# Sending the shift rows of the attention's query stacks from SBUF to SBUF on ScalarE's queue

## The chip, the cores and the metric

One core of a Trainium2 chip runs the whole kernel. The metric is the device time of one execution in microseconds (us); the time before is the median of three runs.

## The reference

The kernel computes a small image tower: a Haar tokenizer, attention with a layer norm, a mixture of eight experts (two per token), a cosine attention block with its feed-forward part, and a second mixture of experts. The change touches only the attention of the first layer, 16 images of 256 tokens with 256 features, 16 heads of 16:

```python
Q, K, V = (proj(Wq, bq), proj(Wk, bk), proj(Wv, bv))
scale = 1.0 / jnp.sqrt(jnp.float32(hd))
scores = jnp.einsum('bhqd,bhkd->bhqk', Q, K) * scale
attn = jax.nn.softmax(scores, axis=-1)
out = jnp.einsum('bhqk,bhkd->bhqd', attn, V)
out = out.transpose(0, 2, 1, 3).reshape(B, S, D)
return out @ Wo.T + bo
```

Its result is added to the input, normed, and routed: logits, the two best experts, a softmax over the two, and each token's rank within its expert.

## The kernel before

The function `attention` runs one image per turn, as a software pipeline of some five turns; all five engines go through the same table `STEPS`, and each takes the steps that it has a function for, in that order. A step's letter gives the image: `n2` is the image of this turn (its load and transpose), `f` the one before (projections), `n` two back (first score pass), `t` three back (second pass, probabilities, values), `p` four back (output projection, norm, routing) and `o` five back (ranks and rows to the experts). So consecutive steps of one engine belong to different images.

The heads are worked in pairs: 8 pairs an image, each with two heads g on partitions 64g and up. q and k are split into a high part and a rest in `parts`; SP writes these to DRAM (`split`, steps qw and kw, L537) and reads them back, stacked three times 16 rows per head, into `qs` and `ks` (`stack`, steps stq and stk, L548): twelve transfers of 128 KB an image, all on SP's queue, the semaphore `stack_in` at the end.

p1_j (L672, TensorE) makes the scores of pair j with 48 rows, queries on the partitions, and VectorE takes their row maximum (L863). After four pairs, step shift_0 or shift_1 (L871, L873, VectorE) makes the negated maxima and their rounding rest. These are to stand in rows 48 and 49 of each query stack, so that the second pass with 50 rows subtracts them. The way there, before: step sw_half transposes them on TensorE into bank[0] (L680), ScalarE copies the 16 x 256 result to `shiftT` (L805), SP writes that to DRAM (`shift_store`, L554) and, in step sr_half, reads it into the stacks (`shift_rows`, L560, two transfers of 8 KB). sw_0 and sr_0 stand late in the turn of p1; sw_1 and sr_1 stand in the next turn.

p2_j (L693, TensorE) makes the scores again, keys on the partitions; p2_0 and p2_4 wait for `shift_in` of their half, and each p2 waits for `prob_ok` of the one before, as the two score banks are one buffer. ScalarE exponentiates (L811). av_k (L705) multiplies with the values; ScalarE copies the result (heads, L818). Routing (step route) is a chain of small VectorE instructions with ScalarE's exponential L834 in it; the ranks follow in step rk (L757 to L761, TensorE, bank[0]). The projections q and k are L650 (q in bank[1], k in bank[0]), with ScalarE's L789 (parts_q, parts_k) behind. Each user of a bank waits for the reader of the use before it (`claim`, `hold`), so who shares bank[0] (rk, sw, k, ot_0) also sets who waits.

Of the kernel before, what the change touches and what calls it, by code (L numbers as in the profile page):

```python
# [6 lines left out]
F32 = mybir.dt.float32  # L7
# [5 lines left out]
ACT = mybir.ActivationFunctionType  # L13
# [3 lines left out]
IMAGES, SEQ, D = 16, 256, 256  # L17
# [15 lines left out]
STACK = 3 * HD  # L33
# [370 lines left out]
def attention(nc, a, s, h0_d, h1_d, rows0_d, ident, before, ones, iota8, cnt, gates0, expert0, rank0, minus_half):  # L404
# [5 lines left out]
    def sb(name, shape, dt=F32):  # L410
        return ctx.enter_context(nc.sbuf_tensor(name, shape, dt))
# [3 lines left out]
    PAIRS = HEADS // 2  # L415
    KROWS = STACK + 2
    RING = 3
# [2 lines left out]
    h0_v = h0_d.rearrange("(i t p) d -> i p t d", t=TPI, p=P)  # L420
    h1_v = h1_d.rearrange("(i t p) d -> i p t d", t=TPI, p=P)
    split_d = [[nc.dram_tensor(f"split_d{u}{n}", (2, 2 * P, SEQ), F32, kind="Internal").ap() for n in "qk"] for u in range(2)]
    shift_d = [nc.dram_tensor(f"shift_d{half}", (2, 2, PAIRS // 2 * SEQ), F32, kind="Internal").ap() for half in range(2)]

    with ctx:
        raw = sb("raw", [P, 4, 2, D])
# [14 lines left out]
        vx = [sb(f"vx{u}", [P, TPI, HEADS, 32]) for u in range(RING)]  # L441
        top = sb("top_a", [P, PAIRS, 2, TPI])
        shift = sb("shift", [P, 2, TPI, 2, 2, PAIRS // 2], F32R)
        shiftT = sb("shiftT", [2 * PAIRS, SEQ])
        prob = sb("prob", [P, 4, 2, TPI, SEQ])
        heads4 = [sb(f"heads4_{u}", [P, SEQ]) for u in range(2)]
        rden = sb("rden", [P, 16])
# [14 lines left out]
        rk = sb("rk", [P, TPI, E])  # L462
# [6 lines left out]
        av_bank = ctx.enter_context(nc.psum_tensor("av_bank", [P, 512], F32))  # L469

        names = ("w_in w_ps w_ok b_in ks_ok bv_ok bo_ps bo_ok filled xt_ps xT_ok q_ps k_ps v_ps qh_ok kh_ok q_ok k_ok v_ok q_out k_out "
                 "s1_ok s1_used shift_ok sT_ps sT_ok sT_out s2_ok prob_ok quad_ok ot_ok on_ps att_ok aT_ps aT_ok o_ps res_ok xb_ok var_ok "
                 "rstd_ok h1_ok hT_ps hT_ok lg_ps lg_ok away_ok ex_ok pick_ok rk_ps rk_ok row_ok").split()
        q = {n: sem("a_" + n) for n in names}
        x_in, h1_out, shift_in = (sem.pair("a_" + n) for n in ("x_in", "h1_out", "shift_in"))
# [3 lines left out]
        def head(k, j):  # L479
            return 8 * (j // 2) + 2 * k + j % 2  # L480

        STEPS = [("ld", "n2"),
# [8 lines left out]

# [11 lines left out]
        with nc.Block() as block:  # L503
            @block.sync
            def _(sp):
                for at, n in enumerate("qkv"):
                    sp.dma_start(raw[:, at], a[f"L0_attn_W{n}"].rearrange("(c p) d -> p c d", p=P)).then_inc(q["w_in"], 16)
                for co in range(2):
                    for ch in range(2):
                        for kk in range(2):  # L510
                            src = a["L0_attn_Wo"][co * P:(co + 1) * P].rearrange("p (hh n r) -> n p hh r", hh=2, r=32)[2 * ch + kk]
                            dst = raw[:, 3, co, ch * P + 64 * kk:ch * P + 64 * kk + 64].rearrange("p (hh r) -> p hh r", hh=2)
                            sp.dma_start(dst, src).then_inc(q["w_in"], 16)
                for n, t in (("q", bq), ("k", bk)):
                    sp.dma_start(t[:], a[f"L0_attn_b{n}"].rearrange("(c p) -> p c", p=P), allow_slow_non_contiguous=True).then_inc(q["b_in"], 16)
                for ch in range(2):
                    for kk in range(2):
                        for hh in range(2):
                            at = 128 * hh + 64 * ch + 32 * kk
                            sp.dma_start(bvT[64 * kk + 32 * hh:64 * kk + 32 * hh + 32, ch:ch + 1],  # L520
                                         a["L0_attn_bv"][at:at + 32].rearrange("(p o) -> p o", o=1)).then_inc(q["b_in"], 16)
                for n, t in (("L0_attn_bo", bo), ("L0_ffn_gate_b", bg)):
                    w = a[n].shape[0]
                    sp.dma_start(t[:], a[n].rearrange("(o d) -> o d", o=1).broadcast_to([P, w])).then_inc(q["b_in"], 16)
                sp.dma_start(wg[:], a["L0_ffn_gate_w"].rearrange("(c p) e -> p c e", p=P)).then_inc(q["b_in"], 16)

                def load(i):
                    if i >= 2:
                        sp.wait_ge(q["xt_ps"], i - 1)
                        sp.wait_ge(q["xb_ok"], i - 1)  # L530
                    sp.dma_start(x[i % 2][:], h0_v[i]).then_inc(x_in[i % 2], 16)

                def split(i, k, n):
                    sp.wait_ge(q[f"{n}_ok"], i + 1)
                    if i >= 2:
                        sp.wait_ge(stack_in[(i - 2) % RING], 16 * 12 * ((i - 2) // RING + 1))
                    sp.dma_start(split_d[i % 2][k].rearrange("a (c p) s -> p a c s", p=P), parts[n][:].bitcast(F32)).then_inc(q[f"{n}_out"], 16)  # L537

                def stack(i, k, n, to, kinds):
                    sp.wait_ge(q[f"{n}_out"], 16 * (i + 1))  # L540
                    if i >= RING:
                        sp.wait_ge(q["s2_ok"], PAIRS * (i - RING + 1))
                    if i == 0:
                        sp.wait_ge(q["ks_ok"], 2 * RING)
                    for b, part in enumerate(kinds):
                        src = split_d[i % 2][k][part].rearrange("(g h f) s -> g f h s", g=2, f=HD)
                        for g in range(2):
                            sp.dma_start(to[i % RING][64 * g + HD * b:64 * g + HD * b + HD].bitcast(F32), src[g]).then_inc(stack_in[i % RING], 16)  # L548

                def shift_store(i, half):  # L550
                    sp.wait_ge(q["sT_ok"], 2 * i + half + 1)
                    if i >= 1:
                        sp.wait_ge(shift_in[half], 32 * i)
                    sp.dma_start(shift_d[half].rearrange("k g (j s) -> (k g j) s", s=SEQ), shiftT[:]).then_inc(q["sT_out"], 16)  # L554

                def shift_rows(i, half):
                    sp.wait_ge(q["sT_out"], 16 * (2 * i + half + 1))
                    at = half * PAIRS // 2
                    for g in range(2):
                        sp.dma_start(qs[i % RING][64 * g + STACK:64 * g + KROWS, at:at + PAIRS // 2].rearrange("p h s -> p (h s)").bitcast(F32),  # L560
                                     shift_d[half][:, g]).then_inc(shift_in[half], 16)

                def store(i):
                    sp.wait_ge(q["h1_ok"], i + 1)
                    sp.dma_start(h1_v[i], h1[i % 2][:]).then_inc(h1_out[i % 2], 16)

                turns({"ld": load, "qw": lambda i: split(i, 0, "q"), "kw": lambda i: split(i, 1, "k"),
                       "stq": lambda i: stack(i, 0, "q", qs, (0, 1, 0)), "stk": lambda i: stack(i, 1, "k", ks, (0, 0, 1)),
                       "sw": shift_store, "sr": shift_rows, "store": store})
                for u in range(2):  # L570
                    sp.wait_ge(h1_out[u], 16 * IMAGES // 2)

# [36 lines left out]
            def _(pe):  # L609
# [74 lines left out]

                def p2(i, j):
                    if j in (0, 4):
                        pe.wait_ge(shift_in[j // 4], 32 * (i + 1))
                    if PAIRS * i + j:
                        pe.wait_ge(q["prob_ok"], PAIRS * i + j)
                    for t in range(TPI):  # L690
                        for g in range(2):
                            rows = slice(64 * g, 64 * g + KROWS)
                            last = nc.tensor.matmul(s2_bank[:, g, t * SEQ:(t + 1) * SEQ], ks[i % RING][rows, j, t * P:(t + 1) * P],  # L693
                                                    qs[i % RING][rows, j, :], start=True, stop=True)
                    last.then_inc(q["s2_ok"], 1)
# [72 lines left out]
            def _(act):  # L768
# [31 lines left out]

                def shift_turn(i, half):
                    act.wait_ge(q["sT_ps"], 2 * i + half + 1)
                    if 2 * i + half:
                        act.wait_ge(q["sT_out"], 16 * (2 * i + half))
                    nc.scalar.activation(shiftT[:], bank[0][0:2 * PAIRS, 0:SEQ], ACT.Copy).then_inc(q["sT_ok"], 1)  # L805

                def p2(i, j):
                    act.wait_ge(q["s2_ok"], PAIRS * i + j + 1)
# [1255 lines left out]
```

## Time and profile before

| | us |
|---|---|
| median of 3 runs | 1855.15 (1852.42 to 1856.64) |
| the profiled execution | 1856.71 |
| its span, first to last instruction | 1855.0 |
| TensorE busy (PE) | 1328.1 (72%) |
| VectorE busy (DVE) | 937.5 (51%) |
| ScalarE busy (ACT) | 512.3 (28%) |
| second score pass L693: idle before, ended by the DMA qs<-shift_d | 44.8 |
| ScalarE's exponentials L811, 128 of 1022 ns | 130.9 |

The attention lies between about 180 and 715 us of the span; the expert stages follow. In the profile PE is TensorE's matmuls, PEld its weight loads, DVE VectorE, ACT ScalarE, POOL GpSimd, SP the sync engine; a q behind an engine's name is its sequencer or queue. PEclk is the granted TensorE clock, 1.00 being 2.4 GHz and 0.50 1.2 GHz. "Idle before" is the time that an engine stood still before an instruction, with what ended it. A turn takes 28 to 30 us.

### The profile page before, as it was taken

The numbers are of one execution on the slowest core, as the hardware profiler recorded it, in microseconds if no ns is written. First come the engines' busy times: TensorE is split into PE (matmuls) and PEld (weight loads), VectorE is DVE, ScalarE is ACT, GpSimd is POOL, SyncE is SP. The second block draws the span as 40 slices with busy tenths as digits, with TensorE's granted clock in tenths as the row PEclk, the third lists the DMA queues.
The fourth block names the chain that finished last, engine by engine and source line by source line (L and its number), as shares of the span: only waits on it lengthen the run. The fifth ranks groups of instructions, "written<-read, shape, count | busy, mean of one in ns | idle before, by whom it ended". The sixth has DMA issues, their size and how long they took to land. (4 is left out here: it accounts for less than half of the span.)

```text
span 1855.0 us, 24280 instructions
## 1 busy us (share of the span) xinstructions
PE 1328.1 (72%) x6868; PEld 916.7 (49%) x6868; DVE 937.5 (51%) x2552; ACT 512.3 (28%) x974; POOL 570.1 (31%) x755
## 2 busy tenths in 40 slices
PE   0001478888889881799999637777777158999996
PEld 0001355555555551566666425555555136667764
DVE  2886346666566642122222257888885204444443
ACT  0000144544444440122222134444343011111111
POOL 7440002221212113000000076677764213333332
PEclk9999688989889765899999857777777578999998
DMA  5012756757566513722222321111100189111110
GB/s 158 23 45 60 125 100 116 143 124 133 129 122 134 102 34 105 246 64 66 66 66 63 80 75 46 46 47 49 51 27 12 49 159 353 34 30 31 33 30 7
DMA packets 134141, 156.92 MB, mean 85 GB/s; under 512 B 25724, under 2 KB 119424, under 8 KB 132992
## 3 DMA queue, kind: packets, MB, share of 16 engines
q1 hardware_dynamic: 121312, 125.88, 28.9%
q0 software_dynamic: 11648, 27.39, 4.5%
q10 hardware_dynamic: 1056, 2.12, 0.5%
q8 instruction: 62, 1.02, 0.2%
q14 instruction: 63, 0.52, 0.1%
HBM read 101.09 MB, written 55.28 MB: 84 GB/s over the span
## 5 line engine op out<-in xcount | busy, mean ns | idle before, releaser
L863 DVE TENSOR_REDUCE top_a<-s_bank 128x4 f32<-128x1024 f32 x128 | 156.5, 1223 | 137.7 <-PE s_bank L672 135.2
L1430 PE MATMUL mbank<-w2T,fhT 128*128 128x256 f32 x512 | 154.8, 469 | 0.0
L811 ACT ACTIVATE prob<-s_bank 128x1024 f32<-128x1024 f32 x128 | 130.9, 1022 | 79.2 <-PE s_bank L693 77.6
L1894 PE MATMUL ebank<-w,exT 128*128 x320 | 148.4, 608 | 0.7 <-ACT exT L1943 0.7
L1905 PE MATMUL ebank<-w,ehT 128*128 x640 | 144.8, 379 | 0.9 <-ACT ehT L1950 0.9
L1430 PEld LDWEIGHTS mbank<-w2T,fhT 128*128 128x128 f32 x512 | 120.2, 241 | 37.4 <-ACT fhT L1537 10.4
L1087 PE MATMUL ebank<-w,exT 128*128 x288 | 137.4, 600 | 0.7 <-ACT exT L1138 0.7
L1098 PE MATMUL ebank<-w,ehT 128*128 x576 | 136.3, 380 | 0.8 <-ACT ehT L1145 0.8
L1905 PEld LDWEIGHTS ebank<-w,ehT 128*128 128x128 f32 x640 | 118.6, 190 | 16.0 <-issue 1.6
L1209 DVE TENSOR_TENSOR eh<-ebank,b 128x512 f32<-128x512 f32 x72 | 49.8, 692 | 145.9 <-PE ebank L1087 145.9
L1098 PEld LDWEIGHTS ebank<-w,ehT 128*128 128x128 f32 x576 | 103.9, 190 | 12.7 <-issue 1.5
L2003 DVE TENSOR_TENSOR eh<-ebank,b 128x512 f32<-128x512 f32 x80 | 55.3, 692 | 101.4 <-PE ebank L1894 100.8
L294 PE MATMUL sums<-part,blocks 128*128 128x10 f32 x8 | 2.3, 361 | 141.7 <-PEq L293 141.7
L693 PE MATMUL s_bank<-qs,ks 50*128 50x256 f32 x512 | 69.0, 351 | 45.8 <-DMA qs<-shift_d 44.8
L599 POOL DMA_INDIRECT rows_d<-h,row_i x64 | 63.3, 989 | 110.6 <-DVE row_i L946 96.0
L1329 POOL IOTA token<- 128x128 int32 x1 | 0.4, 405 | 311.2 <-POOLq L81 311.2
L1894 PEld LDWEIGHTS ebank<-w,exT 128*128 128x128 f32 x320 | 59.4, 196 | 61.0 <-issue 61.0
L672 PE MATMUL s_bank<-ks,qs 48*128 48x256 f32 x512 | 69.8, 355 | 23.6 <-DMA ks<-split_d0k 15.7
L1950 ACT ACTIVATE ehT<-ebank 128x512 f32<-128x512 f32 x80 | 43.5, 595 | 151.9 <-PE ebank L1917 151.8
L705 PE MATMUL av_bank<-prob,vx 128*32 128x256 f32 x1024 | 84.3, 456 | 1.1 <-ACT prob L811 1.1
L588 POOL TENSOR_TENSOR xb<-x,bo 128x512 f32<-128x512 f32 x16 | 20.3, 1272 | 195.3 <-DMA x<-h_d 178.1
L1145 ACT ACTIVATE ehT<-ebank 128x512 f32<-128x512 f32 x72 | 43.0, 597 | 133.2 <-PE ebank L1110 133.2
(324 smaller groups left out, 2568.7 us busy)
## 6 DMA issues: line engine op xcount, KB each, us to landing
w<-in_L_ffn_W SPq DMA_DIRECT2D x16, 1024.0 KB, 11.0
ex<-rows_d SPq DMA_DIRECT2D x72, 128.0 KB, 2.1
y_d<-ey SPq DMA_DIRECT2D x72, 128.0 KB, 1.7
w<-in_L_ffn_w SPq DMA_DIRECT2D x16, 512.0 KB, 5.8
qs<-split_d0q SPq DMA_DIRECT2D x48, 128.0 KB, 5.4
ks<-split_d0k SPq DMA_DIRECT2D x48, 128.0 KB, 5.2
qs<-split_d1q SPq DMA_DIRECT2D x48, 128.0 KB, 4.9
ks<-split_d1k SPq DMA_DIRECT2D x48, 128.0 KB, 4.6
```

What stands on the lines that cost most here:

```text
L599: pool.indirect_dma_start(out=rows0_d, out_offset=bass.IndirectOffsetOnAxis(ap=row_i[i % 2][:, t, k:k + 1], axis=0), in_=h1[i % 2][:, t, : ...
L672: last = nc.tensor.matmul(s1_bank[:, g, t * SEQ:(t + 1) * SEQ], qs[i % RING][rows, j, t * P:(t + 1) * P], ks[i % RING][rows, j, :], start= ...
L693: last = nc.tensor.matmul(s2_bank[:, g, t * SEQ:(t + 1) * SEQ], ks[i % RING][rows, j, t * P:(t + 1) * P], qs[i % RING][rows, j, :], start= ...
L705: last = nc.tensor.matmul(av_bank[32 * j:32 * j + 32, 0:SEQ], vx[i % RING][:, t, head(k, j), :], prob[:, (2 * k + j % 2) % 4, j // 2, t, : ...
L811: nc.scalar.activation(prob[:, j % 4].rearrange("p g t s -> p (g t s)"), s2_bank[:].rearrange("p g s -> p (g s)"), ACT.Exp, scale=HD ** -0 ...
L863: nc.vector.tensor_reduce(top[:, j].rearrange("p g t -> p (g t)"), s1_bank[:].rearrange("p g (t s) -> p (g t) s", t=TPI), axis=AX, op=ALU. ...
L1087: last = nc.tensor.matmul(bank[1 + (FB * j + b) % 2][:], xT[j % 2][:, ch, :], w1[:, bass.ds(e, 1), ch, 512 * b:512 * (b + 1)].rearrange("p ...
L1098: last = nc.tensor.matmul(bank[4 + j % 2][:, 0:D], hT[j % 2][:, f, :], w2[:, bass.ds(e, 1), f, :].rearrange("p a d -> p (a d)"), start=f = ...
L1430: last = nc.tensor.matmul(b[:, t * D:(t + 1) * D], hT[:, f, t * P:(t + 1) * P], w2T[:, f, :], start=False, stop=f == FC - 1)
L1894: last = nc.tensor.matmul(bank[1 + (FB * j + b) % 2][:], xT[j % 2][:, ch, :], w1[:, bass.ds(e, 1), ch, 512 * b:512 * (b + 1)].rearrange("p ...
L1905: last = nc.tensor.matmul(bank[4 + j % 2][:, 0:D], hT[j % 2][:, f, :], w2[:, bass.ds(e, 1), f, :].rearrange("p a d -> p (a d)"), start=f = ...
L2003: nc.vector.tensor_tensor(h[n % HR][:], bank[1 + n % 2][:], b1[:, bass.ds(e, 1), 512 * b:512 * (b + 1)].rearrange("p a f -> p (a f)"), ALU ...
```

## The change

The two transfers through DRAM go, with the tensor `shift_d`, the semaphore `sT_out` and the step sr. ScalarE, which makes `shiftT`, waits for its own copy to be complete and issues four transfers per half straight into the stacks, one for each kind of row and each g: one row of four pairs x 256 from four partitions of `shiftT`. There is one `shiftT` per half. The semaphore of a half is raised by 64 an image instead of 32. The transposes of half 1 (sw_1) move from behind p1_1 to ahead of the rank matmuls. SP has no part in the shift rows any more.

```diff
--- before.py
+++ after.py
@@ -420,7 +420,6 @@
     h0_v = h0_d.rearrange("(i t p) d -> i p t d", t=TPI, p=P)
     h1_v = h1_d.rearrange("(i t p) d -> i p t d", t=TPI, p=P)
     split_d = [[nc.dram_tensor(f"split_d{u}{n}", (2, 2 * P, SEQ), F32, kind="Internal").ap() for n in "qk"] for u in range(2)]
-    shift_d = [nc.dram_tensor(f"shift_d{half}", (2, 2, PAIRS // 2 * SEQ), F32, kind="Internal").ap() for half in range(2)]
 
     with ctx:
         raw = sb("raw", [P, 4, 2, D])
@@ -441,7 +440,7 @@
         vx = [sb(f"vx{u}", [P, TPI, HEADS, 32]) for u in range(RING)]
         top = sb("top_a", [P, PAIRS, 2, TPI])
         shift = sb("shift", [P, 2, TPI, 2, 2, PAIRS // 2], F32R)
-        shiftT = sb("shiftT", [2 * PAIRS, SEQ])
+        shiftT = [sb(f"shiftT{half}", [2 * PAIRS, SEQ]) for half in range(2)]
         prob = sb("prob", [P, 4, 2, TPI, SEQ])
         heads4 = [sb(f"heads4_{u}", [P, SEQ]) for u in range(2)]
         rden = sb("rden", [P, 16])
@@ -469,7 +468,7 @@
         av_bank = ctx.enter_context(nc.psum_tensor("av_bank", [P, 512], F32))
 
         names = ("w_in w_ps w_ok b_in ks_ok bv_ok bo_ps bo_ok filled xt_ps xT_ok q_ps k_ps v_ps qh_ok kh_ok q_ok k_ok v_ok q_out k_out "
-                 "s1_ok s1_used shift_ok sT_ps sT_ok sT_out s2_ok prob_ok quad_ok ot_ok on_ps att_ok aT_ps aT_ok o_ps res_ok xb_ok var_ok "
+                 "s1_ok s1_used shift_ok sT_ps sT_ok s2_ok prob_ok quad_ok ot_ok on_ps att_ok aT_ps aT_ok o_ps res_ok xb_ok var_ok "
                  "rstd_ok h1_ok hT_ps hT_ok lg_ps lg_ok away_ok ex_ok pick_ok rk_ps rk_ok row_ok").split()
         q = {n: sem("a_" + n) for n in names}
         x_in, h1_out, shift_in = (sem.pair("a_" + n) for n in ("x_in", "h1_out", "shift_in"))
@@ -480,12 +479,12 @@
             return 8 * (j // 2) + 2 * k + j % 2
 
         STEPS = [("ld", "n2"),
-                 ("p2_0", "t"), ("av_3", "p"), ("p1_0", "n"), ("xb", "n2"), ("rk", "o"), ("q", "f"), ("rows", "o"), ("qlo", "f"),
-                 ("p2_1", "t"), ("p1_1", "n"), ("sw_1", "t"), ("ot_1", "p"), ("otv_1", "p"), ("k", "f"), ("qw", "f"), ("sr_1", "t"),
+                 ("p2_0", "t"), ("av_3", "p"), ("p1_0", "n"), ("sw_1", "t"), ("xb", "n2"), ("rk", "o"), ("q", "f"), ("rows", "o"), ("qlo", "f"),
+                 ("p2_1", "t"), ("p1_1", "n"), ("ot_1", "p"), ("otv_1", "p"), ("k", "f"), ("qw", "f"),
                  ("p2_2", "t"), ("klo", "f"), ("av_0", "t"), ("p1_2", "n"), ("aT", "p"), ("kw", "f"),
                  ("p2_3", "t"), ("out", "p"), ("p1_3", "n"), ("shift_0", "n"), ("res", "p"), ("stq", "f"),
                  ("p2_4", "t"), ("av_1", "t"), ("v", "f"), ("p1_4", "n"), ("sw_0", "n"), ("nrm", "p"), ("stk", "f"),
-                 ("p2_5", "t"), ("ot_0", "t"), ("p1_5", "n"), ("otv_0", "t"), ("hT", "p"), ("sr_0", "n"),
+                 ("p2_5", "t"), ("ot_0", "t"), ("p1_5", "n"), ("otv_0", "t"), ("hT", "p"),
                  ("p2_6", "t"), ("av_2", "t"), ("p1_6", "n"), ("lg", "p"), ("store", "p"),
                  ("p2_7", "t"), ("xT", "n2"), ("p1_7", "n"), ("shift_1", "n"), ("route", "p")]
 
@@ -547,26 +546,13 @@
                         for g in range(2):
                             sp.dma_start(to[i % RING][64 * g + HD * b:64 * g + HD * b + HD].bitcast(F32), src[g]).then_inc(stack_in[i % RING], 16)
 
-                def shift_store(i, half):
-                    sp.wait_ge(q["sT_ok"], 2 * i + half + 1)
-                    if i >= 1:
-                        sp.wait_ge(shift_in[half], 32 * i)
-                    sp.dma_start(shift_d[half].rearrange("k g (j s) -> (k g j) s", s=SEQ), shiftT[:]).then_inc(q["sT_out"], 16)
-
-                def shift_rows(i, half):
-                    sp.wait_ge(q["sT_out"], 16 * (2 * i + half + 1))
-                    at = half * PAIRS // 2
-                    for g in range(2):
-                        sp.dma_start(qs[i % RING][64 * g + STACK:64 * g + KROWS, at:at + PAIRS // 2].rearrange("p h s -> p (h s)").bitcast(F32),
-                                     shift_d[half][:, g]).then_inc(shift_in[half], 16)
-
                 def store(i):
                     sp.wait_ge(q["h1_ok"], i + 1)
                     sp.dma_start(h1_v[i], h1[i % 2][:]).then_inc(h1_out[i % 2], 16)
 
                 turns({"ld": load, "qw": lambda i: split(i, 0, "q"), "kw": lambda i: split(i, 1, "k"),
                        "stq": lambda i: stack(i, 0, "q", qs, (0, 1, 0)), "stk": lambda i: stack(i, 1, "k", ks, (0, 0, 1)),
-                       "sw": shift_store, "sr": shift_rows, "store": store})
+                       "store": store})
                 for u in range(2):
                     sp.wait_ge(h1_out[u], 16 * IMAGES // 2)
 
@@ -684,7 +670,7 @@
 
                 def p2(i, j):
                     if j in (0, 4):
-                        pe.wait_ge(shift_in[j // 4], 32 * (i + 1))
+                        pe.wait_ge(shift_in[j // 4], 64 * (i + 1))
                     if PAIRS * i + j:
                         pe.wait_ge(q["prob_ok"], PAIRS * i + j)
                     for t in range(TPI):
@@ -800,9 +786,18 @@
 
                 def shift_turn(i, half):
                     act.wait_ge(q["sT_ps"], 2 * i + half + 1)
-                    if 2 * i + half:
-                        act.wait_ge(q["sT_out"], 16 * (2 * i + half))
-                    nc.scalar.activation(shiftT[:], bank[0][0:2 * PAIRS, 0:SEQ], ACT.Copy).then_inc(q["sT_ok"], 1)
+                    if i >= 1:
+                        act.wait_ge(shift_in[half], 64 * i)
+                    nc.scalar.activation(shiftT[half][:], bank[0][0:2 * PAIRS, 0:SEQ], ACT.Copy).then_inc(q["sT_ok"], 1)
+                    act.wait_ge(q["sT_ok"], 2 * i + half + 1)
+                    if i >= RING:
+                        act.wait_ge(q["s2_ok"], PAIRS * (i - RING + 1))
+                    at = half * PAIRS // 2
+                    for k in range(2):
+                        for g in range(2):
+                            row = 64 * g + STACK + k
+                            act.dma_start(qs[i % RING][row:row + 1, at:at + PAIRS // 2].bitcast(F32),
+                                          shiftT[half][8 * k + 4 * g:8 * k + 4 * g + 4, :]).then_inc(shift_in[half], 16)
 
                 def p2(i, j):
                     act.wait_ge(q["s2_ok"], PAIRS * i + j + 1)
```

TensorE's order, at the k projection of a turn, before:

```order
L693 MATMUL s_bank<-qs,ks 128x256 [waits a_prob_ok]
L693 MATMUL s_bank<-qs,ks 128x256 x3
L672 MATMUL s_bank<-ks,qs 128x256 [waits a_s1_used]
L672 MATMUL s_bank<-ks,qs 128x256 x3
L680 MATMUL bank<-ident,shift 16x128 [waits a_rk_ok,a_shift_ok]
L680 MATMUL bank<-ident,shift 16x128
L716 MATMUL bank<-ident,heads_0 128x128 [waits a_xT_ok,a_ot_ok]
L716 MATMUL bank<-ident,heads_0 128x128
L716 MATMUL bank<-ident,heads_1 128x128 x2
L650 MATMUL bank<-xT,wT_k 128x256 [waits a_sT_ok,a_xT_ok]
```

and TensorE's order at the start of the turn, behind p2_0 and av_3, now (lines are 14 lower here; the rank matmuls are L743 to L747, p1 is L658, q is L636):

```order
L658 MATMUL s_bank<-ks,qs 128x256 [waits a_s1_used,a_stack_in1]
L658 MATMUL s_bank<-ks,qs 128x256 x3
L666 MATMUL bank<-ident,shift 16x128 [waits a_att_ok,a_shift_ok]
L666 MATMUL bank<-ident,shift 16x128
L743 MATMUL bank<-both,before 128x8 [waits a_sT_ok,a_pick_ok]
L744 MATMUL bank<-both,before 128x8
L745 MATMUL bank<-both,ones 128x8
L746 MATMUL bank<-both,ones 128x8
L747 MATMUL bank<-both,ones 128x8
L636 MATMUL bank<-xT,wT_q 128x256 [waits a_lg_ok,a_xT_ok]
```

The transposes moved ahead of the rank matmuls, and the wait for ScalarE's copy (sT_ok) moved from the k projection to them.

ScalarE's order late in the turn, around half 0 (vx is the copy of the values, prob the exponential of p2_5), now:

```order
L784 ACTIVATE vx<-bank 128x32x16 [waits a_quad_ok,a_v_ps]
L791 ACTIVATE shiftT<-bank 16x256 [waits a_shift_in0,a_sT_ps]
L799 DMA qs<-shiftT 1x4x256 [waits a_s2_ok,a_sT_ok]
L799 DMA qs<-shiftT 1x4x256 x3
L806 ACTIVATE prob<-s_bank 128x1024 [waits a_quad_ok,a_s2_ok]
L825 ACTIVATE h1T<-bank 128x512 [waits a_lg_ps,a_hT_ps]
```

Before, the exponential stood directly behind the copy to shiftT; now four issues and a wait for the copy stand between them.

SP's order at the stacks, before:

```order
L548 DMA qs<-split_d0q 16x8x256 [waits a_s2_ok,a_q_out]
L548 DMA qs<-split_d0q 16x8x256 x5
L554 DMA shift_d<-shiftT 16x256 [waits a_shift_in0,a_sT_ok]
L548 DMA ks<-split_d0k 16x8x256 [waits a_s2_ok,a_k_out]
L548 DMA ks<-split_d0k 16x8x256 x5
L560 DMA qs<-shift_d 2x1024 [waits a_sT_out]
L560 DMA qs<-shift_d 2x1024
```

The lines L554 and L560 are gone from it now, and the six ks transfers stand directly behind the six of qs.

## Rows read from the trace of the kernel before

**Rows 1.** The page's groups: busy, mean ns, idle before and its releaser

```profile
L693 PE MATMUL s_bank<-qs,ks 50*128 50x256 f32 x512 | 69.0, 351 | 45.8 <-DMA qs<-shift_d 44.8
```

**Rows 2.** Waits, 250 to 760 us: us in total, times, longest us

```profile
PE bank L650 <- ACT shiftT L805: 9.4, 13, 0.7
```

**Rows 3.** Timeline of TensorE in one turn: start, us, instruction, idle before

```profile
487.57 0.50 PE L693 MATMUL s_bank<-qs,ks 50*128 50x256 f32 x4
488.01 1.07 PE L705 MATMUL av_bank<-prob,vx 128*32 128x256 f32 x16
...
491.45 0.50 PE L672 MATMUL s_bank<-ks,qs 48*128 48x256 f32 x4
494.50 0.50 PE L693 MATMUL s_bank<-qs,ks 50*128 50x256 f32 x4 [2.55 <-DMA qs<-shift_d]
494.93 1.63 PE L705 MATMUL av_bank<-prob,vx 128*32 128x256 f32 x16
496.49 0.80 PE L672 MATMUL s_bank<-ks,qs 48*128 48x256 f32 x4
497.22 0.19 PE L757 MATMUL bank<-both,before 128*128 128x8 bf16 x1
```

**Rows 4.** The same turn, SP's queue

```profile
486.19 2.74 SPq L548 DMA_DIRECT2D ks<-split_d0k  x6
...
488.97 0.59 SPq L560 DMA_DIRECT2D qs<-shift_d  x2
```

**Rows 5.** The same turn, ScalarE and VectorE

```profile
485.38 0.37 ACT L805 ACTIVATE shiftT<-bank 16x256 f32<-16x256 f32 x1 [0.15 <-PE bank L680]
...
485.81 1.02 ACT L811 ACTIVATE prob<-s_bank 128x1024 f32<-128x1024 f32 x1
...
492.00 1.23 DVE L863 TENSOR_REDUCE top_a<-s_bank 128x4 f32<-128x1024 f32 x1 [1.22 <-PE s_bank L672]
...
494.58 0.22 ACT L834 ACTIVATE ex<-away 128x16 f32<-128x16 f32 x1 [2.09 <-DVE away L922]
...
496.61 0.38 ACT L818 ACTIVATE heads<-av_bank 128x256 f32<-128x256 f32 x1 [0.54 <-PE av_bank L705]
```

**Rows 6.** Last maximum and rk, first and last of 13 turns

```profile
286.81 1.22 DVE L863 TENSOR_REDUCE top_a<-s_bank 128x4 f32<-128x1024 f32 x1 [1.22 <-PE s_bank L672]
...
292.53 0.19 PE L757 MATMUL bank<-both,before 128*128 128x8 bf16 x1
...
637.55 1.22 DVE L863 TENSOR_REDUCE top_a<-s_bank 128x4 f32<-128x1024 f32 x1 [0.60 <-PE s_bank L672]
...
644.09 0.19 PE L757 MATMUL bank<-both,before 128*128 128x8 bf16 x1
```

**Rows 7.** Issues of two lines: ns min/median/max, first and last start us

```profile
L560 SPq DMA_DIRECT2D qs<-shift_d x64: 223/255/740, 226.4 to 679.0; - x64
...
L234 ACTq DMA_DIRECT2D weight<-in_L_tok_Wa x4: 419/441/844, 3.7 to 5.1; - x4
```

**Rows 8.** Windows: busy PE, PEld, DVE, ACT, POOL; clock, DMA share, GB/s

```profile
256.00:258.00 2.00, 0.00 (x0) 0.00 (x0) 0.00 (x0) 0.00 (x0) 0.00 (x0) 0.59 1.17 123
...
487.00:494.00 7.00, 4.96 (x48) 3.40 (x48) 4.94 (x11) 3.36 (x5) 0.00 (x0) 1.00 1.06 163
...
496.00:498.00 2.00, 2.00 (x19) 1.20 (x12) 0.60 (x1) 0.45 (x2) 1.08 (x1) 0.50 0.00 0
...
523.00:529.00 6.00, 6.00 (x36) 3.74 (x37) 4.18 (x18) 1.62 (x3) 1.62 (x2) 0.50 0.02 6
```

**Rows 9.** Timeline of TensorE: the two first pauses before p2_0

```profile
232.11 0.80 PE L693 MATMUL s_bank<-qs,ks 50*128 50x256 f32 x4 [4.70 <-DMA qs<-shift_d]
...
259.45 0.80 PE L693 MATMUL s_bank<-qs,ks 50*128 50x256 f32 x4 [5.73 <-DMA qs<-shift_d]
```

## The prediction

> **What bounds the kernel now.** I read the page's groups first, then the waits, then the order of time of single turns, then windows.
>
> The page's group of the second score pass (p2, L693) shows the stall that the change aims at: 44.8 of its 45.8 us of idle time end with the transfer qs<-shift_d [rows 1]. In order of time it is one pause of TensorE per turn, before p2_0, 15 times: two first ones of 4.70 and 5.73 us [rows 9] and 13 others of (44.8 - 10.4) / 13 = 2.6 on average. The waits add a smaller one: 13 times TensorE waits for ScalarE's shiftT, 9.4 us in all or 0.72 each, before the k projection, since both use bank[0] [rows 2].
>
> TensorE in the turn at 480 to 508 [rows 3]: p1_7 runs to 491.95, p2_0 starts at 494.50 after 2.55 us idle, then come av_3, p1_0 and at 497.22 the rank matmuls rk. The queue explains the pause [rows 4]: SP sends six ks transfers from 486.19 to 488.93 and the two shift rows behind them, to 489.56. TensorE goes on 4.9 us later.
>
> But TensorE is not the only chain that runs to rk. VectorE and ScalarE in the same turn [rows 5]: the last maximum starts at S = 492.00, shift and routing follow on VectorE, and ScalarE's routing exponential (L834, 0.22) starts at 494.58, S + 2.58, released by VectorE. ScalarE takes its steps in order, so the exponential of p2_0 can't start before about S + 2.8, whenever the shift rows land.
>
> **The change, step by step.**
>
> A. *The pause before p2_0 goes; what is late next.* The rows are issued by ScalarE right behind the copy to shiftT, which in this turn ends at 485.75 [rows 5], at about 486.9 rather than 489.56. A landing of the same 4.9 us would be 491.8, just before p1_7 ends. So p2_0, av_3 and p1_0 move up. Then the transposes of shift_1 now stand ahead of rk, and rk needs bank[0] back from ScalarE's copy of them. ScalarE's chain from S: 2.58, exponential of the routing 0.22, of p2_0 1.02, heads copy 0.38, shiftT copy 0.37, some 0.1 of semaphores: rk starts at S + 4.7 [rows 5]. Before, rk started 5.72 after S in the first such turn and 6.54 in the last [rows 6]; the mean of the 13 is 5.70. So this gives 1.0 a turn, 13 turns: -13 us. Most of the pause of 2.6 us comes back as a pause in front of rk.
>
> B. *k projection.* Its wait of 0.72 goes, since bank[0] is then held by rk, long read. The two transposes no longer stand there either: I take 0.3 us for them (a small pair of matmuls), since ahead of rk they are under the wait of A. 13 x 1.0 = -13 us. The cover of this is the pause of A; gone, it costs 0.3 a turn.
>
> C. *ScalarE's DMA issues.* Eight an image, no engine time in the page, but ScalarE stands for each. The nearest rows are SP's own for the same rows: 223 / 255 / 740 ns, and the only issues of ScalarE, at the program's start: 419 / 441 / 844 ns [rows 7]. I take SP's, since they are the same rows at the same place: 4 x 0.26 + 0.1 = 1.1 us. For half 1 they stand behind the shiftT copy and before parts_q, which waits for eight q matmuls anyway: nothing. For half 0 they stand before the exponential of p2_5, at 485.81 [rows 5]. It would end 1.1 later than 486.83; p2_6 starts at 487.57 [rows 3], so 0.7 is hidden and 0.4 to 0.5 stays. 15 x 0.45 = +7 us. Bounds: 0 below, and at 0.74 each (3.1 - 0.7) x 15 = 36 above.
>
> D. *The clock.* Behind the pause the granted clock falls to 0.50, the 1.2 GHz level, for some 3 us (496 to 498 is inside it) or 7 us (523 to 529) [rows 8]. Before that fall TensorE had stood still for 2.55 us, and been busy ahead of it. While it is low av_3 takes 1.63 rather than 1.07, and p1_0 0.80 rather than 0.50 [rows 3]; in a long spell all of av_3 and p2_0 too. These lie in the 5.70 of A. After the change the pause stands about 2.2 us later, from p1_0 and the transposes (about S + 2.2) to S + 4.7, some 2.5 us, about as long as before. So I expect the spell as well, beginning later, and its price on rk's followers (q, p2_1, p1_1). What A took out comes back there: 0.9 in short, 1.5 in long spells, 1.15 x 13 = +15 us. Bounds: 0 (the spells stay where ScalarE bounds) and 15.
>
> E. *The two first pauses*, 4.70 and 5.73 us [rows 9], have no routing chain behind. But p1_0 needs all twelve stack transfers, and the DMA engines are full (share 1.17) until 258 [rows 8]. In the second, p1_0 came at 259.45 + 0.7 + 1.9 = 262.0 behind p2_0 and a slow av_3; it can now start when the stacks are there, some 258.6: -3.4. In the first I allow 0.7 for the same reason and 1.5 for the k wait (B's kind, with ScalarE behind an exponential): together -5.6 us. Bounds 0 and 10.4.
>
> F. *SP's queue* loses three transfers and two waits per half; the ks stack no longer waits for shiftT and is issued where the qs burst ends. The engines, 1.06 busy in 487 to 494 [rows 8], get it some 2 us earlier. In a steady turn nobody waits for it: nothing. It only protects p1_0 after A. The second shiftT buffer removes a wait that was never long. POOL: nothing moved past it.
>
> Sum: -13 - 13 + 7 + 15 - 5.6 = **-10 us**. The profiled execution took 1856.7 us (span 1855.0), 1.6 above the median of 1855.15. So 1846 against it, and **1845 us** against the median.
>
> The one rule to weigh: here the shift rows landed 4.9 us after their issue, behind six 128 KB transfers of their own queue [rows 4]. The Trainium skill, page "DMA: Bandwidth & Descriptors", section "Issuing engines are not separate DMA queues", says that transfers of all issuing engines run on the same 16 DMA engines and interleave, so that a second issuer saves only issue time. The trace of before has no second such queue to show it; it speaks for the second rival below, and by it the sum would be some 4 us smaller.
>
> **Rivals.**
>
> 1. *The low clock goes or shortens.* For: the pause gets somewhat shorter on average, 2.5 for 2.6, and its place among the busy stretches changes. Against: a pause of 2.55 brought a fall [rows 3, 8]. A spell of 3 to 7 us costs half its length, about 2.4; without any, 13 x 2.4 = 31 us less: 1814.
>
> 2. *The rows land only with the burst, whoever issues them.* The ks burst ends near 492 in the turn shown; p2_0 would start there, and it has time until about 493.8, as ScalarE's chain of A stays the later one. So steady turns keep their gain, but the first two pauses give back some 4 us: 1849. It decides if landing takes over 7 us from 486.9; then each further us costs one.
>
> 3. *ScalarE's issues cost more: slower.* Each pass behind half 0 delays p2_5's exponential, and p2_6 waits for it. The sum is zero when 15 times the rest is 17, that is at 0.44 us an issue. ScalarE's own rows at the start have a median of 0.441 and the slowest of SP's 0.74 [rows 7]. For: those rows are ScalarE's, and SP is issuing the stacks near that time. Against: SP's rows in place are 0.26. At 0.53 it gives 1859, at 0.74 1874.
>
> 4. *The pause only moves*: ScalarE's chain takes longer than S + 4.7, with 0.25 us more between each of its four instructions (gaps that these rows of a waiting engine can't show), rk comes at S + 5.7 as before, and A gives nothing: 1845 + 13 = 1858.
>
> **How the numbers follow.** Forecast (1838 to 1852) 0.52; rival 1 0.12; rival 2 0.10; rival 3 0.15, of which a third lands near no change; rival 4 0.11. A difference of 0.2%, 3.7 us, is about what measurements of this kernel can tell. Faster by more (below 1851.4): nearly all of the forecast, rival 1 and a part of 2: 0.66. Within: 0.19. Slower: 0.15. The range leaves out most of rival 1 (0.08) and the worse half of rival 3 (0.07), with a little of the bounds of C and D: 1822 to 1863.
>
> **What would show it.** In the profile after: no L679 group waiting for a DMA (right for A), instead 2 to 2.6 us idle before the rank matmul L743, released by ScalarE's shiftT; rk at S + 4.7; no wait before k (B); four ACTq issues of 0.26 each, and p2_6 waiting 0.4 for prob (C); the granted clock of 223 to 650 as before (D). Wrong if: waits for qs<-shiftT remain (rival 2), issues of 0.44 or more (3), PEclk clearly up (1), or rk at S + 5.7 (4).

## The result, and the profile after

The change made the kernel slower: 1882.29 us median (fastest 1879.17) against 1853.79 before, ratio 1.0148, 95% interval 1.0127 to 1.0168. The forecast was 1845 us, the range ended at 1863.

The profile taken with that result was a disturbed execution (2004 us, with a lower clock in all stages), so the profile shown here is that of the same kernel taken again in the first experiment, 1880.4 us, span 1878.7. Its page's group of p2 (L679, before L693) (behind the bar: busy time and mean ns of one, then the idle time before them and what ended it) and, from the view of ScalarE's issuing line, what one issue takes (shortest/median/longest, in ns):

```profile
L679 PE MATMUL s_bank<-qs,ks 50*128 50x256 f32 x512 | 73.2, 371 | 36.8 <-ACT prob L806 29.1
```

```profile
L799 ACTq DMA_DIRECT2D qs<-shiftT x128: 580/580/1194, 221.9 to 695.0; - x128
```

The stall for qs<-shift_d, 44.8 us in [rows 1], is gone, and one of 29.1 us for `prob` has taken its place. An issue takes 0.58 us, not the 0.255 of [rows 7]. TensorE's waits, 250 to 760 us (total, times, longest):

```profile
PE s_bank L679 <- ACT prob L806: 29.1, 18, 2.4
PE bank L743 <- ACT shiftT L791: 12.9, 14, 1.8
...
PE s_bank L679 <- DMA qs<-shiftT: 2.9, 2, 2.6
```

The k projection waits no more [rows 2]; the rank matmuls L743 do. All of TensorE's waits of this view, without the one for `ex<-rows_d` of the stage behind the attention, add up to 66.9 us before and 60.5 after: TensorE stands less than before, and yet the kernel is slower. One turn of all engines in order of time, which answers to [rows 3] to [rows 5]; S is the start of its last maximum, 504.35:

```profile
493.53 0.37 ACT L791 ACTIVATE shiftT<-bank 16x256 f32<-16x256 f32 x1 [0.15 <-PE bank L666]
493.93 2.41 ACTq L799 DMA_DIRECT2D qs<-shiftT  x4
...
496.44 1.02 ACT L806 ACTIVATE prob<-s_bank 128x1024 f32<-128x1024 f32 x1 [2.54 <-issue]
...
497.52 0.50 PE L679 MATMUL s_bank<-qs,ks 50*128 50x256 f32 x4 [1.72 <-ACT prob L806]
...
503.51 0.79 PE L658 MATMUL s_bank<-ks,qs 48*128 48x256 f32 x4
...
504.11 0.63 PE L679 MATMUL s_bank<-qs,ks 50*128 50x256 f32 x4
504.35 1.22 DVE L858 TENSOR_REDUCE top_a<-s_bank 128x4 f32<-128x1024 f32 x1 [3.07 <-PE s_bank L658]
504.66 1.93 PE L691 MATMUL av_bank<-prob,vx 128*32 128x256 f32 x16
...
508.73 0.17 PE L743 MATMUL bank<-both,before 128*128 128x8 bf16 x1 [0.88 <-ACT shiftT L791]
508.84 3.06 PEld L636 LDWEIGHTS bank<-xT,wT_q 128*128 128x128 f32 x8
```

The reader is to see three things. p2_0 (504.11) follows p1_7 at once: the pause of 2.55 us is gone. ScalarE's four issues take 2.41 us, the exponential of p2_5 starts 2.54 late, and p2_6 stands for 1.72. And soon after that stop everything on TensorE runs at half clock: p2_7, p2_0 and av_3 (1.93 where it was 1.63), p1_0 and q. The windows of that turn show it (columns as in [rows 8]):

```profile
494.00:497.00 3.00, 1.72 (x12) 1.13 (x12) 2.90 (x6) 0.56 (x1) 0.12 (x1) 1.00 1.15 120
...
499.00:509.00 10.00, 9.12 (x60) 5.92 (x56) 5.56 (x21) 3.73 (x8) 1.27 (x1) 0.50 0.43 76
509.00:512.00 3.00, 3.00 (x9) 2.36 (x8) 1.19 (x9) 0.00 (x0) 1.26 (x2) 0.50 0.02 5
```

Over 280 to 640 us the granted clock is 0.81, before it was 0.90. First the kernel before, then the change:

```profile
280.00:640.00 360.00, 312.44 (x2422) 206.06 (x2420) 229.50 (x643) 171.05 (x283) 73.62 (x84) 0.90 0.66 128
```

```profile
280.00:640.00 360.00, 322.64 (x2292) 211.94 (x2292) 212.94 (x611) 161.82 (x269) 71.85 (x81) 0.81 0.65 118
```

Read in windows of one microsecond, the low spells (the stretches at 0.50) add up to 73 us before and 137 us after, in 360 and 372 us; they were 3.4 or 6.8 us long (the last 10.2), now mostly 10.2 to 17 (two of 6.8, one of 3.4). While TensorE is what the rest waits for, a spell costs half its length: the 64 us more are worth 32 us at most, and 32 less the 6 us by which the waits shrank is about what the kernel lost (28).

### The profile page after: what moved, and what is told of

Read it like the earlier page. It is cut to its first block and busy times, and to the rows that moved or that the text cites. A ratio compares the mean times of both kernels' runs of the same rounds, so it can differ in the third digit from the quotient of the medians.

```text
span 2002.4 us, 24306 instructions
## 1 busy us (share of the span) xinstructions
PE 1491.0 (74%) x6868; PEld 976.4 (49%) x6868; DVE 930.4 (46%) x2552; ACT 511.8 (26%) x974; POOL 570.4 (28%) x755
## 5 line engine op out<-in xcount | busy, mean ns | idle before, releaser
L1889 PE MATMUL ebank<-w,exT 128*128 x320 | 171.0, 685 | 0.7 <-ACT exT L1938 0.7
L1900 PE MATMUL ebank<-w,ehT 128*128 x640 | 167.4, 422 | 0.8 <-ACT ehT L1945 0.8
L1425 PE MATMUL mbank<-w2T,fhT 128*128 128x256 f32 x512 | 167.6, 500 | 0.0
L1082 PE MATMUL ebank<-w,exT 128*128 x288 | 158.3, 679 | 0.7 <-ACT exT L1133 0.7
L1093 PE MATMUL ebank<-w,ehT 128*128 x576 | 156.8, 422 | 0.8 <-ACT ehT L1140 0.8
L1900 PEld LDWEIGHTS ebank<-w,ehT 128*128 128x128 f32 x640 | 124.6, 199 | 30.4 <-issue 1.7
L1093 PEld LDWEIGHTS ebank<-w,ehT 128*128 128x128 f32 x576 | 109.6, 199 | 23.7 <-issue 1.7
L679 PE MATMUL s_bank<-qs,ks 50*128 50x256 f32 x512 | 75.7, 381 | 37.9 <-ACT prob L806 29.6
L691 PE MATMUL av_bank<-prob,vx 128*32 128x256 f32 x1024 | 95.9, 508 | 1.1 <-ACT prob L806 1.1
L658 PE MATMUL s_bank<-ks,qs 48*128 48x256 f32 x512 | 77.0, 387 | 23.0 <-DMA ks<-split_d0k 15.6
L658 PEld LDWEIGHTS s_bank<-ks,qs 48*128 48x128 f32 x512 | 49.7, 238 | 75.2 <-issue 46.2
```

The source lines that it names most:

```text
L658: last = nc.tensor.matmul(s1_bank[:, g, t * SEQ:(t + 1) * SEQ], qs[i % RING][rows, j, t * P:(t + 1) * P], ks[i % RING][rows, j, :], start= ...
L691: last = nc.tensor.matmul(av_bank[32 * j:32 * j + 32, 0:SEQ], vx[i % RING][:, t, head(k, j), :], prob[:, (2 * k + j % 2) % 4, j // 2, t, : ...
L1082: last = nc.tensor.matmul(bank[1 + (FB * j + b) % 2][:], xT[j % 2][:, ch, :], w1[:, bass.ds(e, 1), ch, 512 * b:512 * (b + 1)].rearrange("p ...
L1093: last = nc.tensor.matmul(bank[4 + j % 2][:, 0:D], hT[j % 2][:, f, :], w2[:, bass.ds(e, 1), f, :].rearrange("p a d -> p (a d)"), start=f = ...
L1425: last = nc.tensor.matmul(b[:, t * D:(t + 1) * D], hT[:, f, t * P:(t + 1) * P], w2T[:, f, :], start=False, stop=f == FC - 1)
L1889: last = nc.tensor.matmul(bank[1 + (FB * j + b) % 2][:], xT[j % 2][:, ch, :], w1[:, bass.ds(e, 1), ch, 512 * b:512 * (b + 1)].rearrange("p ...
```

## The experiments

Theory T1: ScalarE's issues hold back p2_5's exponential and the low clock follows. Rival T2: moving half 1's transposes ahead of the rank matmuls costs the time. Every run stands beside runs of the kernel before on the same chip (1850.7 to 1851.8 us median); the ratio is to these.

**1. The change again.**

> The changed kernel, unaltered, for a profile that is not disturbed. Theory T1 (ScalarE's issues: about 0.6 us each, 2.4 us a half, hold back the exponential of p2_5, TensorE stops before p2_6 and the low clock follows there): 1880 us; ScalarE's issue rows at a median near 0.58 us; TensorE waits for prob before p2_6 for 1.2 to 1.8 us a turn, 15 times; rank matmuls 4.3 to 4.7 us after the start of the last maximum. Rival T2 (the pause in front of the rank matmuls, made by moving the transposes of half 1, costs the time): that pause is longer than the one before p2_6 and rk comes 5.7 us or more after the last maximum.

Measured: 1881.7 us, ratio 1.0148 (1.0099 to 1.0197). T1's rows are there: 0.58 us an issue, 1.72 us of waiting before p2_6, and the rank matmuls come at S + 4.38. The stop before them, 0.9 us in most turns, is shorter than p2_6's. That speaks for T1 but prices neither.

**2. SP issues the same transfers.** The loop of four `dma_start` moves from ScalarE's `shift_turn` to a `shift_rows` of SP, ahead of the ks stack (only the lines that change owner are shown):

```diff
-                            act.dma_start(qs[i % RING][row:row + 1, at:at + PAIRS // 2].bitcast(F32),
+                            sp.dma_start(qs[i % RING][row:row + 1, at:at + PAIRS // 2].bitcast(F32),
...
-                       "store": store})
+                       "sw": shift_rows, "store": store})
```

> The same eight transfers from SBUF to SBUF, at the same place in the order, but issued by SP, ahead of the ks stack; ScalarE only copies. T1: ScalarE's exponential of p2_5 directly behind the copy again, no wait of TensorE for prob before p2_6: 1835 to 1850 us. It also prices an issue of this shape on SP: near 0.26 us if ScalarE's engine makes it dear, near 0.6 if the shape (one row from four partitions) does. T2: ScalarE's issues don't matter: 1875 to 1885 us.

Measured: 1852.58 us, ratio 0.9991 (0.9966 to 1.0016): 29 us less than the change and as long as before; T1 had said 1835 to 1850, T2 1875 or more. The wait for `prob` is 3.9 us in all, and the low spells add up to 72 us in 280 to 640, as before. An issue costs the same 0.57 us here, so the engine doesn't make it dear. SP issues the ks stack 2.4 us later, and TensorE now waits for that before p1_0:

```profile
L557 SPq DMA_DIRECT2D qs<-shiftT x128: 572/573/1177, 224.5 to 669.4; - x128
```

```profile
PE s_bank L669 <- DMA ks<-split_d1k: 19.6, 7, 3.2
PE s_bank L669 <- DMA ks<-split_d0k: 19.3, 7, 4.5
```

**3. The order alone.** The kernel before, with

```diff
-                 ("p2_0", "t"), ("av_3", "p"), ("p1_0", "n"), ("xb", "n2"), ("rk", "o"), ("q", "f"), ("rows", "o"), ("qlo", "f"),
-                 ("p2_1", "t"), ("p1_1", "n"), ("sw_1", "t"), ("ot_1", "p"), ("otv_1", "p"), ("k", "f"), ("qw", "f"), ("sr_1", "t"),
+                 ("p2_0", "t"), ("av_3", "p"), ("p1_0", "n"), ("sw_1", "t"), ("xb", "n2"), ("rk", "o"), ("q", "f"), ("rows", "o"), ("qlo", "f"),
+                 ("p2_1", "t"), ("p1_1", "n"), ("ot_1", "p"), ("otv_1", "p"), ("k", "f"), ("qw", "f"), ("sr_1", "t"),
```

> The kernel before with one edit: the transposes of half 1 stand ahead of the rank matmuls; the rows go through DRAM on SP's queue as before, two issues each. T1: the move costs little or gains: the k wait of 9.4 us goes, and the rank matmuls wait for ScalarE's copy instead: 1845 to 1860 us. T2: the move alone makes it slower: 1870 us or more.

Measured: 1867.53 us, ratio 1.0084 (1.0061 to 1.0107). This lies between the two expectations, nearer T2's, which I had not believed: the order alone costs 16 us. The timeline of a turn shows a new stop of only 0.56 us, before L757:

```profile
502.00 0.79 PE L693 MATMUL s_bank<-qs,ks 50*128 50x256 f32 x4 [2.42 <-DMA qs<-shift_d]
502.73 1.93 PE L705 MATMUL av_bank<-prob,vx 128*32 128x256 f32 x16
504.59 0.79 PE L672 MATMUL s_bank<-ks,qs 48*128 48x256 f32 x4
505.32 0.59 PE L680 MATMUL bank<-ident,shift 128*16 128x128 f32 x2
506.46 0.17 PE L757 MATMUL bank<-both,before 128*128 128x8 bf16 x1 [0.56 <-ACT shiftT L805]
```

The k wait it removes is 0.72, so the waits balance: all of them in 250 to 760 us add up to 67.0 us, before 66.9. But in one-microsecond windows each of the twelve low spells is 10.2 us, 123 us in 374; the mean clock over 280 to 640 is 0.83. So here the waits can't be what costs the 16 us, and the clock can: 50 us more at half clock are 25 us at most.

**4. Half 0's issues later, two and two.** In ScalarE's order two go behind the h1T copy, two behind the heads copy of av_2.

> The changed kernel, but for half 0 ScalarE issues two of the four transfers only behind the exponential of p2_5 and the h1T copy, and two behind the heads copy of av_2, where it stood idle before; half 1 as in the change. T1: 1.2 us in each place instead of 2.4 in one, mostly under idle time of ScalarE: TensorE's waits for prob shrink to under 0.5 us a turn: 1840 to 1860 us, unless the last rows land too late for p2_0. T2: the number of issues on ScalarE is the same, and so is the pause at the rank matmuls: 1875 to 1885 us.

Measured: 1879.04 us, ratio 1.0134 (1.0084 to 1.0185), in T2's range. The waits for `prob` fell to 3.3 us as said, but the rows landed late: TensorE waits for them in 14 turns.

```profile
PE s_bank L679 <- DMA qs<-shiftT: 55.2, 14, 6.7
```

So the time doesn't tell the two theories apart; the "unless" of T1's expectation came true.

**5. The order alone, without the stop.** Run 3 suggests theory T3: the small stop behind the pause keeps the clock low; rival T4 is that the transposes' new place does it. In the third kernel half 1's transposes go to bank[2]:

```diff
-                    claim(0)
+                    claim(2 * half)
...
-                    hold[0] = (q["sT_ok"], 2 * i + half + 1)
+                    hold[2 * half] = (q["sT_ok"], 2 * i + half + 1)
...
-                    nc.scalar.activation(shiftT[:], bank[0][0:2 * PAIRS, 0:SEQ], ACT.Copy).then_inc(q["sT_ok"], 1)
+                    nc.scalar.activation(shiftT[:], bank[2 * half][0:2 * PAIRS, 0:SEQ], ACT.Copy).then_inc(q["sT_ok"], 1)
```

> The third experiment (order alone, rows through DRAM) with the transposes of half 1 in bank[2] instead of bank[0], so that the rank matmuls don't wait 0.55 us for ScalarE's copy. Theory T3 (what the move costs is the low clock: the 0.55 us stop behind the pause before p2_0 keeps every spell at 10.2 us, 123 us low in 374 against 73 in 360 before): without that stop the spells are 3.4 to 6.8 us again, low in all under 85 us, and the time is 1840 to 1856. Rival T4 (the transposes' own place, not the stop, costs it): still 1863 to 1870 and spells of 10.2 us.

Measured: 1832.38 us, ratio 0.9884 (0.9842 to 0.9926): 35 us less than run 3, and below T3's range. The stop before the rank matmuls, 7.8 us in 14 turns, is gone, and the wait before p2_0 is 36.6 us for 42.3; all waits add up to 53.4, 13.6 less than in run 3. The spells are 3.4 and 6.8 us (the last 17.1), 79 us low in 360 where run 3 has 123, clock 0.89: 44 us less at half clock are 22 at most, and 22 + 13.6 is about the 35. T3 holds, T4 falls. It is also 19 us faster than the kernel before: the order is good once the bank isn't shared.

**6. The change, without that stop.** The same edit to the changed kernel.

> The changed kernel with the transposes of half 1 in bank[2]. The stop of about 0.9 us before the rank matmuls goes, the one of 1.7 us before p2_6 (ScalarE's four issues) stays. T3, if the two stops together make the spells long: low clock falls from 137 us to under 100, time 1860 to 1872. T5 (the stop before p2_6 alone does it): 1876 to 1884, low clock above 125.

Measured: 1863.98 us, ratio 1.0061 (1.0036 to 1.0086), 18 us less than the change. The time is that of T3; the low clock, 123 us in 360, is above the 100 that T3 had said and just under T5's 125. What stays is p2_6's stop, and with it the long spells. So ScalarE's issues (run 2, 29 us) and the shared bank (this run, 18 us) are both causes; neither alone.

**7. The rows ahead of the last two ks transfers**, in the kernel before: step stk sends four, a new step behind sr_0 the last two (the new parameter of `stack` isn't shown).

```diff
-                 ("p2_5", "t"), ("ot_0", "t"), ("p1_5", "n"), ("otv_0", "t"), ("hT", "p"), ("sr_0", "n"),
+                 ("p2_5", "t"), ("ot_0", "t"), ("p1_5", "n"), ("otv_0", "t"), ("hT", "p"), ("sr_0", "n"), ("stl", "f"),
...
-                       "stk": lambda i: stack(i, 1, "k", ks, (0, 0, 1)),
+                       "stk": lambda i: stack(i, 1, "k", ks, (0, 0, 1), (0, 1)), "stl": lambda i: stack(i, 1, "k", ks, (0, 0, 1), (2,)),
```

> The kernel before with one edit in SP's order: the two shift-row transfers of half 0 go ahead of the last two of the six ks stack transfers instead of behind all six. The pause before p2_0 was said to come from the rows' place in the queue. If so: p2_0 waits 1.0 to 1.8 us less, p1_0 may wait for the stack instead, rk can start up to 1.5 us earlier: 1830 to 1850 us. If the landing takes 4.9 us whatever is ahead of it: within 3 us of before, 1849 to 1855.

Measured: 1822.61 us, ratio 0.9839 (0.9799 to 0.9879), better than said. The wait for the rows is 18.0 us in 14 turns (before 40.1 in that window), and the clock 0.92:

```profile
PE s_bank L695 <- DMA qs<-shift_d: 18.0, 14, 3.7
```

**8. The change with half 0's issues by SP, half 1's by ScalarE, and bank[2].**

> The change with half 0's four transfers issued by SP ahead of the ks stack, half 1's by ScalarE, and half 1's transposes in bank[2]. No stop before p2_6 and none before the rank matmuls; what stays is the wait of p1_0 for the ks stack (2.3 to 3.2 us with SP issuing both halves). T3: as all with SP issues or better, 1838 to 1853. If ScalarE's issues of half 1 hurt (they stand before parts_q): 1856 or more.

Measured: 1843.18 us, ratio 0.9944 (0.992 to 0.9967). ScalarE's issues of half 1 don't hurt; the wait for `prob` is 7.4 us, and p1_0 waits 35 us in all for the ks stack.

**9. The two edits that helped** (runs 5 and 7) together.

> The kernel before (rows through DRAM on SP) with the two edits that helped: half 0's rows ahead of the last two ks transfers, and half 1's transposes ahead of the rank matmuls in bank[2]. The first gave 29 us, the second 19; if the low clock spells shrink further they add up in part: 1795 to 1818 us, low clock under 55 us in 360. If they took away the same loss: 1818 to 1825.

Measured: 1806.41 us, ratio 0.9773 (0.9735 to 0.981). The gains of 19 and 29 us add up to 44. This is the fastest kernel of the study, and its rows still go through DRAM on SP's queue. Over 280 to 640 its clock is 0.92, with 55 us at half clock:

```profile
280.00:640.00 360.00, 334.69 (x2714) 219.94 (x2707) 254.65 (x727) 190.10 (x313) 82.53 (x95) 0.92 0.64 132
```

It does 2714 matmuls in that stretch, where the kernel before did 2422 and the change 2292.

**10. Rows ahead of the last four.**

> As the one before it, with the rows of half 0 ahead of the last four ks transfers. SP may then stand up to 0.5 us for the DRAM write, and p1_0 waits for the stack instead: within 6 us of the one before it. Clearly faster (over 6 us) only if the rows still landed late there.

Measured: 1809.86 us, ratio 0.9791 (0.9771 to 0.981): not to be told from run 9. The rows' wait is nearly gone (1.3 us) and one of 14.4 us for the ks stack stands in its place.

**11. Half 0 shared, two issues each, bank[2].** ScalarE takes `for k in (0,)`, SP `for k in (1,)`.

> The change with half 1's transposes in bank[2] (the sixth run, 1864 us), and of half 0's four transfers two issued by ScalarE and two by SP. T1 (the stop before p2_6 is 2.4 us of issues less some 0.7 hidden): with 1.2 us of issues it is 0.4 to 0.6 us instead of 1.7, low clock under 100 us, 1838 to 1852 us. If ScalarE's issues aren't the cause: 1860 us or more.

Measured: 1824.47 us, ratio 0.9872 (0.9835 to 0.9909), 40 us less than run 6 and below the range that I had said. The stop before p2_6 is 0.5 to 0.8 us in most turns (said 0.4 to 0.6) where it was 1.7, and the wait for `prob` falls from 31.7 to 18.1 us. All waits add up to 42.0 us for 50.5, since p1_0 now waits 7 us for the ks stack; the low spells, 85 us in 360 for 123, are worth 19 more at most. So T1's mechanism holds, but its amount isn't settled: 8.5 and 19 leave some 12 of the 40 us unexplained. The kernel beats the one before. That doesn't show that rows from SBUF to SBUF are worth anything: run 5 has the same order and bank with the rows through DRAM, and its ratio of 0.9884 (0.9842 to 0.9926) can't be told from this one.

**12. What makes an issue dear.**

```diff
-                            act.dma_start(qs[i % RING][row:row + 1, at:at + PAIRS // 2].bitcast(F32),
-                                          shiftT[half][8 * k + 4 * g:8 * k + 4 * g + 4, :]).then_inc(shift_in[half], 16)
+                            to = qs[i % RING][row:row + 1, at:at + PAIRS // 2].bitcast(F32)
+                            src = raw[row:row + 1, 0:2]
+                            if half == 0:
+                                act.dma_start(to, src.rearrange("p a b d -> p (a b) d")).then_inc(shift_in[half], 16)
+                            else:
+                                act.dma_start(to.rearrange("p h s -> p (h s)"), src.rearrange("p a b d -> p (a b d)")).then_inc(shift_in[half], 16)
```

> What makes an issue cost 0.58 us. The change, but the rows' source is one partition of a weight tile (so the rows hold weights instead of the negated maxima and their rest, and the probabilities are others): in half 0 both sides are 1 x 4 x 256, in half 1 both are 1 x 1024. If the four partitions of the source make it dear, both lines show 0.26 us; if the four pieces do, half 0 shows 0.58 and half 1 0.26; if it is any transfer from SBUF to SBUF, both show 0.58.

Measured, one run: 1884.36 us. The two lines' issues, and for half 0 the time from issue to landing:

```profile
L802 ACTq DMA_DIRECT2D qs<-raw x64: 504/611/1742, 223.1 to 688.1; - x64
...
DMA to landing us min/median/max: 1.7/8.0/10.2
```

```profile
L804 ACTq DMA_DIRECT2D qs<-raw x64: 504/611/1862, 234.9 to 702.4; - x64
```

Both halves show 0.61 us, so neither the source's four partitions nor the number of pieces makes the issue dear. What the dear issues have in common is both ends in SBUF and a single row as destination; which of the two counts wasn't tried. The 255 ns of [rows 7] were for a transfer from DRAM to two rows of SBUF.

## Why the prediction was wrong

The forecast sum was -10 us, the measured difference +28: 38 us are to be explained, and two terms failed, C and D.

**C failed: the price of an issue.** It took 0.26 us an issue "since they are the same rows at the same place". They are the same rows, but not the same transfer. The measured 0.58 gives by the prediction's own arithmetic 4 x 0.58 + 0.1 - 0.7 = 1.7 us a turn, and 1.72 is what p2_6 waits: 15 x 1.7 = 26 us where +7 stood. Rival 3 had the mechanism, its place, and a turning point of 0.44 us; with 0.58 it gives 1845 + 19 = 1864. That is one half of the 38 us, and run 2, which takes the issues off ScalarE, shows that they matter: 29 us.

**D failed: the price of the clock.** For the other half the sum has no other term of that size. Its pauses were to move, with spells as long as before, at a price of 15 us at most; measured are 64 us more at half clock, up to 32 us against the kernel before. The mistake was to count on one long pause a turn, ahead of the rank matmuls: there are two shorter ones, 1.7 us before p2_6 and 0.9 before the rank matmuls, and the spells became mostly 10.2 to 17 us. Rival 1 had the sign of this the other way. Run 5 against run 3 (35 us for 13.6 us less waiting) and run 11 against run 6 (40 for 8.5) show the time falling by two and a half to nearly five times what TensorE stood less; run 3 against the kernel before shows 16 us with no more waiting at all. The bound "0 to 15" had no reason behind its upper end.

**A held in mechanism and nearly in size**: p2_0 came at once, and the rank matmuls at S + 4.38 (said 4.7, before 5.70 in the mean), released by ScalarE's copy at the end of the chain that A adds up. The idle time in front of them was to be 2 to 2.6 us and is 0.9: in the turn shown TensorE is through with the transposes at S + 3.5 rather than S + 2.2, at half clock. Rival 4 falls. But that this wait stands in bank[0] is what runs 3, 5 and 6 price, at 16 to 35 us.

**B held** for the k wait, which is gone; its 0.3 us for the two transposes no run shows alone. **E came in part**: the first pause stayed, 4.60 us for 4.70, the second became 2.62 for 5.73, which is 3.2 us of the 5.6, and the longest of C's waits, 2.45 before p2_6, stands just ahead of it. The change's own profile has no landing of the rows; in run 12, where they are as large and stand at the same place, the median is 8.0 us after the issue, not 4.9. So rival 2 was right on its mechanism, and as it said, the steady turns hid it. The rule of the Trainium skill, "DMA: Bandwidth & Descriptors", section "Issuing engines are not separate DMA queues", agrees with the 8.0 us: another issuer didn't bring the rows past the burst. **F** held: the ks stack was issued earlier, and nobody profited.

What stays open: why a short stop lengthens a spell that has begun. The runs show that spells are longer with the stop and shorter without it; a change in the turn's length, which came with each edit, could have a part in it, and no run holds that fixed.

## What to carry to other kernels

Price a DMA issue by a row with the same kinds of memory at both ends and the same shape, and then ask who stands behind it on the issuing engine: four issues in front of an exponential cost more here than the DRAM hop that they saved. Count the stops of the whole turn, and what the clock did around each: here the sum of the waits fell and the time rose. Where transfers share a queue, first try to change their order: half 0's rows sent ahead of the last two large transfers gave 29 us, with no new transfer at all. And when a step is moved, look at what it now shares a buffer or bank with; the same move cost 16 us in bank[0] and gave 19 in bank[2].

## What the runs showed of the hardware that I had not expected

- An issue of a one-row transfer from SBUF to SBUF takes 0.57 to 0.61 us, on ScalarE (580 ns) and SP (573 ns) alike, whether the source is one partition or four; a transfer from DRAM to two rows takes 0.26 (kernel before).
- Such rows landed 8.0 us (median, run 12) after the issue, beside a burst of the other queue.
- In the kernel before, TensorE's low clock (0.50, 1.2 GHz) lasted 3.4 or 6.8 us (once 10.2) behind one pause of 2.2 to 3.2 us a turn. In run 3 it lasted 10.2 us in all of twelve turns; there a further stop of 0.56 us stood 3.9 us behind the pause.
